# Edge attention of a graph network: block columns from tables of ready products, one semaphore signal per four sums, eight buffers of gathered rows instead of four

## What is computed

```python
rows, cols = edge_index            # src, dst
q = (embeds[rows] @ qTrans).reshape(e, h, hd)
k = (embeds[cols] @ kTrans).reshape(e, h, hd)
v = (embeds[cols] @ vTrans).reshape(e, h, hd)
att = jnp.clip(jnp.einsum('ehd,ehd->eh', q, k), -10.0, 10.0)
expAtt = jnp.exp(att)
attNorm = segment_sum(expAtt, rows, n)[rows]
res = segment_sum((expAtt / (attNorm + 1e-08))[:, :, None] * v, rows, n) + embeds
out = layernorm(res) * ln_scale + ln_bias
```

## Time and profile before

| | us |
|---|---|
| three runs, median | 7215.49 |
| lowest and highest | 7204.37, 7318.86 |
| the profiled execution | 7202.38 |
| its span, first to last instruction | 7200.5 |
| edge attention: first gather to last `weigh` | 5692.1 to 7111.1 |
| PE, DVE, ACT, POOL busy over the span | 5138.8, 5824.7, 3716.2, 3967.3 |

### The profile page before, as it was taken

The page is one execution under the profiler, slowest core; times in us unless marked ns, Lnnn a source line. Parts: engine busy times, 40 slices in busy tenths (PEclk is TensorE's granted clock), DMA queues, the critical chain, the costliest instruction groups (busy, mean ns, idle before and its releaser), DMA issues. The chain is left out here.

```text
span 7200.5 us, 128816 instructions
## 1 busy us (share of the span) xinstructions
PE 5138.8 (71%) x22244; PEld 2877.3 (40%) x22245; DVE 5824.7 (81%) x13976; ACT 3716.2 (52%) x17417; POOL 3967.3 (55%) x3546
## 2 busy tenths in 40 slices
PE   3386589972588898988877889889885555445452
PEld 2254233321244444444443444444443344444442
DVE  9596899972599999999848999999996455555556
ACT  5142500001399999999738999999993200000000
POOL 0688868882266666656305665666650255555552
PEclk9975899985799999999989999999997776776765
DMA  0234000001355555555424555555560233333333
GB/s 12 31 66 47 6 1 1 1 3 41 113 138 139 138 140 140 140 138 139 77 71 130 139 139 139 139 138 140 139 126 21 79 95 97 96 97 97 98 96 59
DMA packets 397679, 657.24 MB, mean 91 GB/s; under 512 B 141671, under 2 KB 259365, under 8 KB 396947
## 3 DMA queue, kind: packets, MB, share of 16 engines
q0 software_dynamic: 185888, 481.62, 27.2%
q1 hardware_dynamic: 211442, 172.59, 9.9%
HBM read 617.73 MB, written 33.88 MB: 90 GB/s over the span
## 5 line engine op out<-in xcount | busy, mean ns | idle before, releaser
L1209 POOL DMA_INDIRECT feat_area<-xl_table,feat_area x1856 | 1984.9, 1069 | 1721.1 <-PE bank L1283 680.1
L1360 ACT ACTIVATE feat_area<-feat_area 128x130 f32<-128x130 f32 x5568 | 1642.7, 297 | 181.2 <-issue 119.3
L1270 PE MATMUL bank<-node_area,feat_area 128*128 x3712 | 1470.2, 519 | 353.8 <-DVE feat_area L1405 158.5
L1344 ACT ACTIVATE feat_area<-feat_area 128x128 f32<-128x128 f32 x4640 | 1443.0, 387 | 64.6 <-issue 64.4
L1283 PE MATMUL bank<-feat_area 128*128 128x390 f32 x3712 | 1408.5, 502 | 68.1 <-ACT feat_area L1344 21.8
L1772 POOL DMA_INDIRECT feat_area<-kv_table,feat_area x832 | 809.8, 973 | 899.7 <-DVE feat_area L1869 352.5
L600 POOL DMA_INDIRECT rec_by_dst<-feat_area,gather_col x800 | 1123.0, 1404 | 281.3 <-issue 240.1
L1360 ACT ACTIVATION_READ_ACCUMULATOR feat_area<-feat_area 128x1 f32 x5568 | 1040.0, 187 | 26.9 <-issue 26.4
L1270 PEld LDWEIGHTS bank<-node_area,feat_area 128*128 128x128 f32 x3712 | 637.4, 191 | 997.9 <-issue 732.5
L1405 DVE TENSOR_TENSOR feat_area<-bank,feat_area 128x780 f32<-128x780 f32 x928 | 886.0, 955 | 65.1 <-remote 41.0
L1283 PEld LDWEIGHTS bank<-feat_area 128*128 128x128 f32 x3712 | 666.6, 190 | 645.8 <-issue 246.3
(11 more groups left out here) (313 smaller groups left out, 6762.8 us busy)
## 6 DMA issues: line engine op xcount, KB each, us to landing
feat_area<-lo_slot SPq DMA_DIRECT2D x464, 128.0 KB
feat_area<-xl_table,feat_area POOLq DMA_INDIRECT x1856
feat_area<-lo_slot_src SPq DMA_DIRECT2D x208, 128.0 KB
node_area<-lo_edge SPq DMA_DIRECT2D x100, 256.0 KB
xl_table<-feat_area SPq DMA_DIRECT2D x98, 195.0 KB, 2.2
feat_area<-kv_table,feat_area POOLq DMA_INDIRECT x832
rec_by_dst<-feat_area,gather_col POOLq DMA_INDIRECT x800
feat_area<-gates SPq DMA_DIRECT2D x348, 32.0 KB
```

Source lines behind the costliest of these rows:

```text
L1209: pool.indirect_dma_start(ring[:, at:at + HE], None, k.xl, bass.IndirectOffsetOnAxis(ap=index[s // CG][:, n:n + 1], axis=0)).then_inc(gath ...
L1270: last = nc.tensor.matmul(pair[s % 2][:, u, 0:HE], pick[s // 2 % 2][:, c:c + P], k.node[:, ds(columns[0], HE)], start=True, stop=True)
L1344: last = nc.scalar.activation(row[:, 0:D], row[:, 0:D], ACT.Copy, scale=row[:, D:D + 1])
L1360: last = nc.scalar.activation(at, at, ACT.Copy, accum_out=score[s // CG][:, to:to + 1])
```

## The change

It does three things in `edge_attention`.

1. SP loads the block number of each of the 832 tiles (`block_s`) into one partition. DVE converts them to float and writes two tables of products, `q_col` = block x 128 and `acc_col` = block x 136. `tile_columns` then loads columns from them straight into registers: PE 4 words a group, DVE 16 words each fourth group. `block_words` and `block_columns` are no longer used.
2. The last of a group's four matmuls in `sums` alone signals `summed`, which now counts groups. All waits for it change with that: DVE waits once, in `find_columns`, for all four sums of the group instead of for each sum before its addition.
3. U is 8 instead of 4: eight `kv`, `lo_bc` and `index` buffers, and eight groups in a turn of the loop.

```diff
+def tile_columns(k, engine, table, tile, n, width):
+
+    return k.nc.values_load_multi_w_load_instructions(
+        table[0:1, ds(tile, n)], engines=(engine,), min_val=0, max_val=(NB - 1) * width,
+        skip_runtime_bounds_check_because="every block was limited to NB - 1 before it was multiplied")[1]
...
-    U = 4
+    U, B = 8, 8
     cut = Carver(k.wide)
-    kv = [cut(G * KV) for _ in range(U)]
+    kv = [cut(G * KV) for _ in range(B)]
...
+    of_tile = cut(T_SRC, I32, 1)
+    block_f, q_col, acc_col = cut(T_SRC, F32, 1), cut(T_SRC, I32, 1), cut(T_SRC, I32, 1)
...
+            sp.dma_start(of_tile, k.block_s[0:T_SRC].rearrange("(o t) -> o t", o=1)).then_inc(loaded, 16)
+
             def load(j, s):
...
+            pe.wait_ge(columns_set, 1)
+
             def look(j, s):
                 g = U * j + s
-                columns = block_columns(pe, block_words(k, PE, g, 1)[0], range(G), D)
+                columns = tile_columns(k, PE, q_col, g * G, G, D)
...
                 for u in range(G):
-                    nc.tensor.matmul(k.bank[2 + u][:, 0:VW], place[s % 2][:, u * P:(u + 1) * P],
-                                     wv[s % 2][:, u * VW:(u + 1) * VW], start=True, stop=True).then_inc(summed, 1)
+                    last = nc.tensor.matmul(k.bank[2 + u][:, 0:VW], place[s % 2][:, u * P:(u + 1) * P],
+                                            wv[s % 2][:, u * VW:(u + 1) * VW], start=True, stop=True)
+                last.then_inc(summed, 1)
...
-                    act.wait_ge(summed, G * g - G)
+                    act.wait_ge(summed, g - 1)
...
+            do = Order(dve, order)
+            dve.wait_ge(loaded, 16)
+            do(nc.vector.tensor_copy(block_f, of_tile))
+            do(nc.vector.tensor_scalar(q_col, block_f, float(D), None, ALU.mult))
+            nc.vector.tensor_scalar(acc_col, block_f, float(VW), None, ALU.mult).then_inc(columns_set, 1)
+            dve.wait_ge(columns_set, 1)
             nc.vector.memset(acc, 0.0).then_inc(cleared, 1)
...
             def places(j, s, g):
-                first = snapped(dve, g * G)
                 if later(g, 2):
-                    dve.wait_ge(summed, first - G)
-                key_rows(k, place[s % 2], k.lo_src, first, G)
+                    dve.wait_ge(summed, g - 1)
+                key_rows(k, place[s % 2], k.lo_src, snapped(dve, g * G), G)
...
-            words, columns, tile = [], [], []
+            columns = []
 
             def find_columns(j, s, g):
-                if s == 0:
-                    words[:] = block_words(k, DVE, U * j, U)
-                columns[:] = block_columns(dve, words[s], range(G), VW)
-                tile[:] = [snapped(dve, g * G)]
+                if s % 4 == 0:
+                    columns[:] = tile_columns(k, DVE, acc_col, g * G, 4 * G, VW)
+                dve.wait_ge(summed, g + 1)
 
             def add(u):
                 def fn(j, s, g):
-                    dve.wait_ge(summed, tile[0] + (u + 1))
                     if u > 0 or later(g):
-                        dve.wait_ge(added, tile[0] + u)
-                    to = acc[:, ds(columns[u], VW)]
+                        dve.wait_ge(added, g * G + u)
+                    to = acc[:, ds(columns[s % 4 * G + u], VW)]
                     nc.vector.tensor_tensor(to, to, k.bank[2 + u][:, 0:VW], ALU.add).then_inc(added, 1)
```

More of the change, by code:

```diff
@@ L1757, in edge_attention @@
     index = [cut(G, I32) for _ in range(U)]
+    of_tile = cut(T_SRC, I32, 1)
+    block_f, q_col, acc_col = cut(T_SRC, F32, 1), cut(T_SRC, I32, 1), cut(T_SRC, I32, 1)
     gathered = [k.gather_sem(f"f_gathered{s}") for s in range(U)]
     index_set, lo_ready = ([k.sem(f"f_{n}{s}") for s in range(U)] for n in ("index", "lo"))
+    loaded, order, columns_set = k.sem("f_loaded"), k.sem("f_order"), k.sem("f_columns")
     names = ("cleared", "picked", "looked", "mult", "att", "clip", "exp", "weighed", "summed", "added")
```

## The result

The changed kernel took 7286 us (median of 7 runs, 7261 to 7309), the kernel before beside it 7229 us (7 runs, 7185 to 7319). The ratio is 1.0102 with an interval of 1.0069 to 1.0135: 1% slower, which is within 2%. The forecast was 7055 us, 2.2% faster, and the range ended at 7230 us. The profiled execution took 7264.7 us with a span of 7262.9 us.

The account below looks back on a forecast made before the run. DVE was taken to pace edge attention, idling in register-instruction stalls under gathers, 2.2 us a group. 166 us saved after shading, less 18 us at the start, gave -148 us: 7055 us, 2.2% below the median; range 6890 to 7230 us.

Parts of the forecast that it names:

- Register instructions: DVE in edge attention: stall goes with the count of register instructions, 2.2 us a group become 1.15.
- the shading: Stall saving in the stage cut to 0.8 us a group, 166 us, as a slow stretch does not shrink by itself.
- One signal for four sums: DVE's first addition waits for all four PE sums: +0.83 us in a group without stalls, bounds 0 and 1.15.
- The sum: Edge attention: 5.87 us a group against 6.78, shaded to 166 us saved, start +18 us, net -148 us.
- Rival B: DVE's stalls under gathers: time alone counts, slow stretch stays 6.5 us per pair; +60 us, 7262 us; 0.27 with C.
- the start: Start of edge attention: +15 us from POOL's longer first row of gathers, +3 us for block loads and tables; +18 us.
- Loads of columns: DVE's 16-word loads each fourth group: between nothing and 0.5 us a group, taken as nothing; PE has time.
- rival C: DVE's 16-word column loads cost 221 ns a word: 104 us later than the forecast, 7159 us; 0.27 together with B.
- Eight buffers: POOL's gathers: depth gives nothing in the steady state; a longer first row costs +15 us at the start.
- Rival D: POOL's gathers: deeper buffers bring long rows again and again, 7.9 us a group, 7450 us; 0.08 with other slower ways.
- Rival A: DVE in edge attention: the stalls go altogether, 5.2 us a group, 6890 us; 0.20 with all up to 7000 us.

Follow-up runs that it names:

- q1_each_between: Changed kernel with four semaphores, one signal per sum, and DVE's order multiply, reduce, addition 0, places, addition 1, clip, addition 2, picks, addition 3, weigh; 7249.8 us, 1.0 of before.
- runs with pauses: Unread 4608-number reduce added ahead of every second group's multiplication: before 7072.5 us, changed 7201.9, changed with four signals 7061.5, changed with later additions 7197.6.
- e3_depth: Kernel before with eight buffers instead of four, nothing else; 6847.6 us, 0.9995 of the kernel before.
- e7_each_later: Changed kernel with four signals, one per sum, and DVE's additions after multiply, reduce and places; 6811.1 us, 0.9939 of the kernel before.
- a_third: The changed kernel, unchanged, run again in a session without stalls; 6838.8 us, 0.9983 of the kernel before.
- q2_each_between_paused: Changed kernel with four signals, DVE's additions each one place later, and an unread reduce ahead of every second group's multiplication; 7246.9 us, 0.9979 of the kernel before.
- b_again: The kernel before, unchanged, profiled again in a session without stalls; 6838.8 us, 1.0001 of the kernel before.
- changed kernel with pauses: Changed kernel with an unread reduce of 4608 numbers ahead of every second group's multiplication; 7201.9 us, against 7072.5 us for the kernel before with the same pauses.

## Why the prediction was wrong

**Register instructions: the step that failed.** "If the stall goes with their count, 2.2 us a group become 2.2 x 14/27 = 1.15." It doesn't. In the result a stalled group is 4.87 us longer than an unstalled one, exactly as before; the stalls are rarer, but not shorter. q1_each_between, with the lower count and four signals, bears it out: its groups take 6.75 us (L1889 from 5789.3 to 7185.6 us, 207 intervals) over about 4.0 us without a stall. That is 2.7 us of stall a group, where the kernel before had 6.78 - 4.33 = 2.45. My reading of the earlier trace rows, that the 698 ns are the cost and so their number counts, took a symptom for the cause: in the changed kernel DVE's register instructions stay at 77 ns or less, while its holes of 1.7 and 3.0 us lie between instructions. The earlier trace rows also show two kinds of instruction; the kind of the earlier trace rows took this in the fast stretch:

```profile
L1886 DVEq FUSED_REGOPS  x5: 69/69/75, 6301.1 to 6305.1; - x5
```

This step held the whole gain of the forecast, 1.05 us a group less the shading. q1 shows none of it.

**One signal for four sums: right in kind, mis-sized.** I had +0.83 us in an unstalled group, the mean of 1.15 at the lower clock and 0.5 at the higher. The runs with pauses show 1.35 us (5.58 against 4.23). The value at the lower clock was 0.2 us short, and the mean was the larger error: of the two lines of sums in the earlier trace rows, the quick one (6304.45) lies in the stalled group, whose wait is hidden anyway. In the kernel before, 99 of its 104 unstalled groups have their sums at the lower clock. In the changed kernel 98 unstalled groups at the lower clock take 5.59 us on average, and 38 at the higher 4.91. Under a stall the wait is hidden, as I had it. With real stalls the changed kernel takes 7.04 us a group (L1889 from 5716.7 to 7173.3 us), q1 6.75: 0.29 us a group, 60 us. That is an estimate of the signal's price there, not a measurement, since the two ran in different sessions and q1 has another order on DVE.

**The sum.** In place of 5.98 us a group (6.78 less 0.8) stands 7.04. The profiled executions differ by 62 us, 7264.7 against 7202.4: 23 us are there by the second weighing, and the 206 groups behind it take 38 us longer. Rival B, "time alone counts", gave +60 us and 7262 us. It had the mechanism, a stretch that keeps its length, but its parts are only near: it has 18 us for the start and a stall in every second group, where the stalls now come mostly in every third. That its number fits to 3 us is in part luck, as a kernel's own runs spread by 50 us and more in such a session.

**Loads of columns: right.** 16 words take 1100 ns, 4 take 332 ns, and neither DVE's wait nor the stage's time shows them. That is (1100 - 332) / 12 = 64 ns a further word. The Trainium skill ("Runtime: NRT & Kernel Launch", section "Instruction fetch mechanics") has about 200 ns a register; these rows do not agree, and rival C, with 221 ns a word, falls.

**Eight buffers: nothing without stalls, open with them.** e3_depth took 0.9995 of the kernel before, and POOL is still held by the weighing in the result. Rival D did not come, since POOL does not empty and refill as a block; but its rows grew from mostly 8 gathers to mostly 12, which neither the forecast nor D had. At the start I had +18 us in all, and the second weighing is 23 us later (53.9 against 30.5 us after the first gather).

**Rival A** rested on the stalls' going, and they did not. But in sessions without them both kernels take about 6840 us, so the stalls are worth some 390 us to the kernel before. No edit of this change reaches that.

**What stays open:** what in a session brings the stalls and what holds DVE up in one; and what each part of the change by itself, the one signal or the eight buffers, does under real stalls, since no run of the parts met them.

## What to carry to other kernels

Before a stall is shared out by a count of instructions, ask whether it is a price for each or a stretch of time. Two runs tell together: one with fewer of the instructions, and one with a long harmless instruction in the stretch. If the idle time stays in the first and the time stays in the second, the stretch is what counts, and fewer instructions save nothing. One signal behind several results delays the first reader by nearly the whole batch, at the slower of TensorE's two clocks where the loop has pauses (2.18 us for four sums here, of which 1.35 were paid), so the saved waits must be worth more than that. Of a bound that one execution shows, see whether another session shows it too: here the one in the profile was worth 5% of the time and was gone in four of six sessions. And before two readings of one operation are averaged, see in which kind of group each lies.

The best version found is e7_each_later, four signals and later additions: 0.9939 of the kernel before, and 0.996 of a_third in the same session, without stalls. With stalls nothing run was faster than before.

## What the hardware showed beyond that

The same program took 6840 and 7229 us in different sessions, with a narrow spread in the quick ones (6835 to 6847 us over 25 runs) and a wide one in the others (7209 to 7312 over 19). In the second kind SP's register instructions reach 700 ns and more in the graph layers and the edge attention. DVE's do so in the edge attention of the kernel before alone (up to 1409 ns, L957). In the changed kernel and in q1_each_between they stay short, yet DVE stands still as long: 2.7 us a group in q1. In q2_each_between_paused a DVE instruction of 4.9 us in every second group left the time as it was (7246.9 us, q1 7249.8).

TensorE's granted clock was 0.75 in the stage of b_again (its mean from 5700 to 6600 us) and 0.65 in the changed kernel in the result. PE's four sums take 1.19 us at the higher of its two levels and 2.18 us at the lower. In q2 the two mostly alternate: 2.18 us at 6307.60, after 6.00 us without work, and 1.19 us at 6311.69, after 0.52 us. In the changed kernel with pauses the sums under the pause are at the lower level more often (50 of 103 groups against 13 with four signals): those at 6306.35, after 1.68 us without work, take 2.18 us as well. This lowers the granted clock (0.64 from 5900 to 6900 us, 0.73 with four signals) but not the pace, as DVE is in its pause then. What counts is the level in the groups where DVE waits, and there it was the lower one with either kind of signal.
